# Router logits taken out of the attention's projections, and rows queued without their norm

## The reference, cut to what matters

```python
xn  = layernorm(x)                       # (x - mean) / sqrt(var + 1e-5)
h   = rmsnorm(xn, ln1_w)                 # v * rsqrt(mean(v*v) + 1e-5) * w
q, k, v = split(h @ wqkv.T); rotary on q and k; causal softmax, 16 query and 4 key heads of 16
x2  = xn + attn @ wo.T
h   = rmsnorm(x2, ln2_w)
p   = softmax(h @ gate_w.T)              # 8 experts; the two largest of a token, weights rescaled to sum 1
out = x2 + sum over the token's two experts e of  w_e * (silu(h @ w1_e.T) * (h @ w3_e.T)) @ w2_e.T
x   = x + out
```

## Time and profile before

| | |
|---|---|
| median of 3 runs | 1738.77 us (1736.22 to 1740.03) |
| the profiled execution's own time | 1730.77 us |
| its span (first to last instruction) | 1729.1 us |
| TensorE busy | 1624.7 us, 94% |
| VectorE busy | 1166.1 us, 67% |
| ScalarE busy | 931.3 us, 54% |
| GpSimd busy | 556.0 us, 32% |
| granted TensorE clock, mean | 0.968 |
| routing (stage7) up to the first expert product | 1212.6 to 1345.5 us |
| experts (stage8) | 1345.5 to 1729 us |

### The profile page before, as it was taken

The page is one execution under the profiler, slowest core; times in us unless marked ns, Lnnn a source line. Parts: engine busy times, 40 slices in busy tenths (PEclk is TensorE's granted clock), DMA queues, the critical chain, the costliest instruction groups (busy, mean ns, idle before and its releaser), DMA issues. The chain is left out here.

```text
span 1729.1 us, 29571 instructions
## 1 busy us (share of the span) xinstructions
PE 1624.7 (94%) x9040; PEld 807.7 (47%) x9040; DVE 1166.1 (67%) x3195; ACT 931.3 (54%) x2069; POOL 556.0 (32%) x842
## 2 busy tenths in 40 slices
PE   7899989899999999999999999998995899999996
PEld 3367655333333333334333343332884455565554
DVE  6722788899888888888888888870685344343342
ACT  6134544166676776676676766667573333333332
POOL 3530338163515003030030300000377344444443
PEclk9999999799999999999999999999895899999999
DMA  5000000311030300303003030000378677777774
GB/s 165 1 7 19 2 1 7 62 36 28 2 62 2 62 2 1 62 2 62 2 1 62 2 62 2 1 1 1 120 234 276 122 129 130 131 130 129 129 126 71
DMA packets 252195, 105.77 MB, mean 61 GB/s; under 512 B 208064, under 2 KB 247880, under 8 KB 252040
## 3 DMA queue, kind: packets, MB, share of 16 engines
q1 hardware_dynamic: 233296, 80.62, 22.0%
q0 software_dynamic: 13392, 18.49, 6.3%
q10 hardware_dynamic: 5352, 4.76, 0.8%
HBM read 30.88 MB, written 23.67 MB: 32 GB/s over the span
## 5 line engine op out<-in xcount | busy, mean ns | idle before, releaser
L1677 ACT ACTIVATE prob<-pS 128x512 f32<-128x512 f32 (+3 forms) x1280 | 582.3, 542 | 267.5 <-PE pS L1563 176.2
L1734 DVE TENSOR_REDUCE mx<-pM 128x1 f32<-128x512 f32 x768 | 501.6, 685 | 71.3 <-PE pM L1543 68.1
L1543 PE MATMUL pM<-KT,QT 96*128 96x512 bf16 (+3 forms) x1280 | 434.1, 356 | 16.5 <-DVE mx L1734 5.5
L1559 PE MATMUL pS<-QT,KT 99*128 99x512 bf16 (+3 forms) x1280 | 422.9, 352 | 6.8 <-ACT prob L1677 1.8
L2440 PE MATMUL bank<-w13T,QKV 128*128 x568 | 257.2, 596 | 15.4 <-ACT QKV L2467 15.4
L1730 DVE CUSTOM_DVE_ANT_0 junk<-pM,mask_row 128x128 bf16<-128x128 f32 (+3 forms) x512 | 239.9, 483 | 41.7 <-PE pM L1543 41.1
L1578 PE MATMUL pO<-prob,VV 128*32 128x512 f32 (+3 forms) x2560 | 267.8, 536 | 0.0
L1543 PEld LDWEIGHTS pM<-KT,QT 96*128 96x128 bf16 x1280 | 124.5, 98 | 208.5 <-DVE mx L1734 79.1
L1468 POOL CAST mpart<-mneg 128x16 bf16<-128x16 f32 x32 | 6.8, 213 | 653.9 <-DVE mneg L1742 653.9
L1559 PEld LDWEIGHTS pS<-QT,KT 99*128 99x128 bf16 x1280 | 123.6, 97 | 184.0 <-ACT prob L1677 140.2
L2500 DVE TENSOR_TENSOR QKV<-QKV,bank 128x512 f32<-128x512 f32 x71 | 48.8, 687 | 235.5 <-issue 200.2
(11 more groups left out here) (356 smaller groups left out, 1947.3 us busy)
## 6 DMA issues: line engine op xcount, KB each, us to landing
raw<-in_ffn_w_dram SPq DMA_DIRECT2D x48, 256.0 KB, 4.0
QKV<-queue SPq DMA_DIRECT2D x71, 136.0 KB, 2.5
out_dram<-x ACTq DMA_DIRECT2D x8, 512.0 KB, 4.7
x<-_attn_hidden_states_dram SPq DMA_DIRECT2D x14, 256.0 KB, 5.5
QKV<-QKV SPq DMA_TRANSPOSE x142, 3.2
QT<-mrow SPq DMA_DIRECT2D x128, 3.0 KB
out_dram<-QKV POOLq DMA_INDIRECT x71, 3.9
wc_s<-in_attn_Wc_dram SPq DMA_DIRECT2D x1, 1024.0 KB, 8.1
```

The source lines that it names most:

```text
L1543: last = nc.tensor.matmul(pM[:, bank, 0:w], QT[0:ROWS, par, h, qt * P:(qt + 1) * P], KT[0:ROWS, par, 512 * part:512 * part + w], start=Tru ...
L1559: last = nc.tensor.matmul(pS[:, p % NSC, lo:512], KT[0:ROWS + 3, par, kt * P:(kt + 1) * P], QT[0:ROWS + 3, par, h, 512 * c + lo:512 * c + ...
L1677: nc.scalar.activation(prob[:, n % RING, h, lo:512], pS[:, p % NSC, lo:512], ACT.Exp, scale=SCALE).then_inc(s.head_exp, 1)
L1734: nc.vector.reduce_max(mx[:, h, qt, part:part + 1], pM[:, plan.bank[item], 0:w], AX.X).then_inc(s.unit_max, 1)
```

## The change

It does these things:

1. **The router's logits become eight columns of each projection.** The logits of x2 = xn + attn @ wo.T are xn @ G + attn @ (wo.T @ G), with G the router's weights times the second norm's. G, with its mean taken away, becomes eight columns of `wqkvT` (so that stage6 projects 392 columns), and the product of `wo` with G eight columns of `woT` (so that routing projects 264). stage4 makes both: one product and one subtraction on 8 rows on VectorE, one more `turn_weight` iteration, one iteration with four small products (`output_gate`). A record of `QKV` grows to 392 words. In routing, `routed` on VectorE scales the first part into the last eight columns of `xl`, and the add of 264 columns gives rows and logits at once. `residual_norm` makes the factor for this with two more products on GpSimd.
2. `turn_h`, `h_out` and `logits` are gone, with their PSUM banks and the scaled `gws` of routing. `pX` now has three slots of a bank each, and the add waits tile by tile.
3. **The rows are queued as they are.** `records` is gone. The second norm's weights go into `w13T`: a tile of it is now copied out by two scaled activations (one per half of the channels) in place of one copy. The row's factor `rnorm` travels in the record beside the shares (`tail` is a word wider), is the scale of the silu, and is multiplied into the share.
4. **The lists are one beat shorter** (`LATE` is 10) and ordered anew. The squares of a beat are taken in the same beat, behind its add; the choice is made one beat later instead of two; the weights start one beat earlier. On ScalarE the normalised rows of the next beat stand behind this beat's squares.
5. The broadcast of the second norm's weights at stage6's start is gone; one to eight rows stands in stage4. `xl` lies in the room of `w2T`, so the first tile of `w2T` waits for the last add.

The diff's core (lines that only carry names, sizes or semaphores along are left out):

```diff
@@ stage4
+                nc.vector.tensor_tensor_reduce(scaled[0:E, 3, :], raw[0:E, 5, :], ln2_e[:, :], 1.0, 0.0, ALU.mult, ALU.add,
+                                               wsum[0:E, 0, 3:4]).then_inc(s.w_times, 1)
...
+                nc.vector.tensor_scalar(scaled[0:E, 4, :], scaled[0:E, 3, :], wsum[0:E, 1, 3:4], None,
+                                        ALU.subtract).then_inc(s.w_ready, 1)
...
+                def output_gate():
+                    pe.wait_ge(s.wT_out, 6)
+                    for m in range(C):
+                        for c in range(C):
+                            last = nc.tensor.matmul(pQK[:, 1, m * E:(m + 1) * E], raw[:, 3 + c, m * P:(m + 1) * P],
+                                                    v.gws[:, c, :], start=(c == 0), stop=(c == C - 1))
@@ stage6
-                            last = nc.tensor.matmul(pS[:, t % NSC, 0:QKVW], xT[:, i % 2, j, c, :], wqkvT[:, c, :],
+                            last = nc.tensor.matmul(pS[:, t % NSC, 0:QKVW + E], xT[:, i % 2, j, c, :], wqkvT[:, c, :],
@@ stage7
-    LATE = NQ + 3
+    LATE = NQ + 2
-            per = [0, 0, 4, 4, 4, 4, 4, 4, 8, 8, 8]
+            per = [0, 4, 4, 4, 4, 4, 4, 8, 8, 8]
@@ route_pool
             def scatter(q, first, count):
                 if first == 0:
-                    pool.wait_ge(s.h, G * q + G)
                     pool.wait_ge(s.share, q + 1)
                     pool.wait_ge(s.slots, q + 1)
...
+            for beat in range(LATE):
+                if beat >= 2:
+                    scatter(beat - 2, 0, 4)
+                if beat < NQ:
+                    root2(beat)
+                if beat >= 2:
+                    scatter(beat - 2, 4, 4)
@@ route_pe
             def project(i):
                 pe.wait_ge(s.aT_out, i + 1)
-                if i >= 2:
-                    pe.wait_ge(s.x2, 2 * i - 2)
                 for j in range(2):
+                    t = 2 * i + j
+                    if t >= SX:
+                        pe.wait_ge(s.x2, t - SX + 1)
                     for c in range(C):
-                        last = nc.tensor.matmul(pX[:, 2 * (i % 2) + j, :], aT[:, i % 2, j, c, :], v.woT[:, c, :],
+                        last = nc.tensor.matmul(pX[:, t % SX, :], aT[:, i % 2, j, c, :], v.woT[:, c, :],
...
-                    if 1 <= beat <= NQ:
-                        turn_h(2 * (beat - 1) + j)
...
-                    if 1 <= beat <= NQ:
-                        logits(2 * (beat - 1) + j)
...
-                if 2 <= beat <= NQ + 1:
+                if beat >= 2:
                     ranks(beat - 2)
                 turn_weights(ws[3 * quarter:])
-                if beat == 3:
+                if beat == 2:
                     spare_tokens()
@@ route_act
+                        for c in range(C):
+                            last = nc.scalar.activation(
+                                w13T[:, c, 2 * P * n:2 * P * (n + 1)].rearrange("p (a n) -> p a n", a=2), src[:, c],
+                                ACT.Copy, scale=v.ln2c[:, c:c + 1])
...
-                for j in range(2):
-                    if beat < NQ:
-                        attended_out(2 * beat + j)
-                    if 1 <= beat <= NQ:
-                        h_out(2 * (beat - 1) + j)
-                    weights_out(ws[j * quarter:(j + 1) * quarter])
-                    if j == 0 and 2 <= beat <= NQ + 1:
-                        exponential(beat - 2)
-                    if j == 0 and beat < NQ:
-                        normal(beat)
+                if beat < NQ:
+                    attended_out(2 * beat)
+                if beat == 0:
+                    normal(0)
+                weights_out(ws[0:quarter])
+                if beat < NQ:
+                    attended_out(2 * beat + 1)
+                weights_out(ws[quarter:2 * quarter])
+                if beat < NQ:
+                    squares(beat)
                 if 1 <= beat <= NQ:
-                    squares(beat - 1)
+                    exponential(beat - 1)
                 weights_out(ws[2 * quarter:3 * quarter])
+                if beat + 1 < NQ:
+                    normal(beat + 1)
...
                 weights_out(ws[3 * quarter:])
@@ route_dve
+                nc.vector.tensor_tensor(QKV[:, t, 0:H + E], xl[:, t % G, :], pX[:, t % SX, :], ALU.add).then_inc(s.x2, 1)
+
+            def routed(q):
+                four = slice(G * q, G * q + G)
+                if q >= 1:
+                    dve.wait_ge(s.x2, G * q)
+                nc.vector.tensor_tensor(xl[:, :, H:H + E], QKV[:, four, ROUTED:ROUTED + E], bc(v.norm1[:, 0, four]),
+                                        ALU.mult).then_inc(s.routed, 1)
...
-                if 2 <= beat <= NQ + 1:
-                    soften(beat - 2)
-                    records(beat - 2)
-                    choose(beat - 2)
-                if beat == 4:
+                if beat == 3:
                     spare_out()
                 if beat < NQ:
                     attended(beat)
-                if 2 <= beat <= NQ + 1:
+                if beat + 1 < NQ:
+                    routed(beat + 1)
+                if 1 <= beat <= NQ:
+                    soften(beat - 1)
+                if beat >= 2:
                     settle(beat - 2)
                 if beat == 2:
                     spare_hot()
+                if 1 <= beat <= NQ:
+                    choose(beat - 1)
                 if beat < NQ:
                     residual(beat)
@@ stage8
         def silu(j):
             act.wait_ge(s.half, j + 1)
+            act.wait_ge(s.tail_in, j + 1)
             if j >= 2:
                 act.wait_ge(s.gated, j - 1)
-            nc.scalar.activation(sil[:, j % 2, :], pH[:, j % 2, 0, :], ACT.Silu).then_inc(s.sil, 1)
+            nc.scalar.activation(sil[:, j % 2, :], pH[:, j % 2, 0, :], ACT.Silu,
+                                 scale=share[:, j % RT, E + 1:E + 2]).then_inc(s.sil, 1)
```

More of the change, by code:

```diff
@@ L44 @@
 QKVW = (NH + 2 * NKV) * HD
+ROUTED = QKVW
 E = 8
@@ L852, in weight_rows @@
         def weight_rows(n):
-            return E if n == 5 else P
+            return E if n >= 5 else P
         with nc.Block() as block:
@@ L932, in turn_weight @@
                         pe.wait_ge(s.wT_out, n - 1)
-                    src = scaled[:, n, :] if n < 3 else raw[0:rows, n, :]
+                    src = scaled[:, n, :] if n < 3 else raw[:, n, :] if n < 5 else scaled[0:rows, n - 2, :]
                     for c in range(C):
@@ L1795, in stage7 @@
     NQ = T // G
-    LATE = NQ + 3
+    LATE = NQ + 2
     R = 4
+    SX = 3
     RP = 3
@@ L1933, in route_pool @@
             pool.wait_ge(s.ids_in, 2)
-            for beat in range(1, LATE):
-                if beat >= 3:
-                    scatter(beat - 3, 0, 4)
-                if beat <= NQ:
-                    root2(beat - 1)
-                if beat >= 3:
-                    scatter(beat - 3, 4, 4)
+            for beat in range(LATE):
[5 more added lines that the diff above has]
+                    scatter(beat - 2, 4, 4)
             pool.wait_ge(s.acc_in, 16 * NQ)
@@ L2157, in soften @@
                 nc.vector.tensor_tensor(pr[:, :, :], lg[:, :, :], bc(red[:, 0, :]), ALU.subtract).then_inc(s.soft, 1)
-            def records(q):
-                dve.wait_ge(s.square, G * q + G)
-                dve.wait_ge(s.rstd2, q + 1)
-                dve.wait_ge(s.hT_mm, 2 * q + 2)
-                dve.wait_ge(s.resid, q + 1)
-                for t in range(G * q, G * q + G):
-                    nc.vector.scalar_tensor_tensor(out=QKV[:, t, 0:H], in0=QKV[:, t, 0:H],
-                                                   scalar=rstd[:, 4, t:t + 1], in1=v.ln2_b[:, :], op0=ALU.mult,
-                                                   op1=ALU.mult).then_inc(s.h, 1)
             def choose(q):
@@ L2235, in route_dve @@
             nc.vector.memset(prior[:, 0, :], 0.0).then_inc(s.prior0, 1)
[L2236 to L2239 removed]
+            routed(0)
             for beat in range(LATE):
[L2241 to L2245 removed]
+                if beat == 3:
                     spare_out()
@@ L2355, in stage8 @@
     xq, xqT = carve(R, REC), carve(2, C * P)
-    tail = carve(RT, E + 1).bitcast(I32)
+    tail = carve(RT, E + 2).bitcast(I32)
     share = tail.bitcast(F32)
```

149 lines of the change are left out of this document (65 added, 84 removed).

## The result

The changed kernel takes 1752.46 us (median of five, 1750.69 to 1758.83); the kernel before, beside it, 1736.97 us. The ratio is 1.0090, with a 95% interval of 1.0069 to 1.0111: 12 to 19 us slower. The forecast was 1750.2 us (1739 to 1760), slower with 0.78. The profiled execution is the first of the five (1752.84 us, span 1751.1).

A forecast was written before the change was run, and what follows sets the result against it. POOL's scatter queue was taken as the bound, overtaken by a new ScalarE-TensorE loop of 13.25 us a beat. The last scatter came 10.9 us later, plus 0.5 in attention: 1738.77 + 11.4 = 1750.2 us, range 1739 to 1760.

The forecast's parts named there:

- What bounds: Routing: POOL's queue of 64 scatters ends last, 11.7 us a beat; the experts' stage only moves as a whole.
- Rival 4: Routing: the squares' wait is in truth covered and the change moves nothing, 1738.8 us; chance 0.03.
- rival 1: Routing: POOL stays the bound because the clock holds and the loop is 11.5 us; 1738.9 to 1742 us; chance 0.20.
- The loop: Routing: ScalarE and TensorE take turns instead of overlapping, 11.5 us a beat, 13.25 with the lowered clock.
- only then the copy: ScalarE's queue: next attended tiles are copied only behind squares, exponential, rows and two weight tiles; TensorE waits, idling nearly 5 us.
- Its size: Loop per beat: ScalarE's part 6.05 us, TensorE's 5.45, lowered clock 1.75; together 13.25 us.
- Rival 2: Routing: TensorE stays at half clock through its whole part, a beat of 15.6 us, 1764 us; chance 0.10.
- Rival 1's rule: Routing: removed records, with two SBUF inputs, no longer contend with POOL's reads, giving the lower end, 1738.9 us.
- Beat 3: Routing: spare-token products ahead of this beat's transposes add 1.3 us, last add at 1258.8 us.
- The tail: Routing's end: from beat 5's scatters POOL bounds, 11.7, 10.2 and 8.9 us, last scatter starting at 1345.7 us.
- rival 3: Routing's end: tables end last, their ranks standing behind 46 weight tiles; 2 to 6 us more, 1752 to 1756; chance 0.05.
- What was costed at nothing: Silu's scale and wait, router's product and small transposes, and work removed from TensorE, ScalarE and VectorE: 0 us directly.

The follow-up runs named there:

- e4: Kernel before with only ScalarE's order taken from the change (squares of the same beat, next beat's normalised rows behind them): 1758.45 us, ratio 1.0119.
- e10: Changed kernel with only ScalarE's list reordered: weight tiles and next attended copy ahead of the squares; spare-token products left in place: 1744.17 us, ratio 1.0059.
- e9: Changed kernel, ScalarE's weight tiles and next attended copy ahead of the squares, spare-token products behind the fifth beat's first transposes: 1738.65 us, ratio 1.0015.
- e1: Changed kernel with ScalarE's copy of the next beat's first two attended tiles ahead of this beat's squares: 1757.20 us, ratio 1.0120.
- e7: Changed kernel with both lists regrouped: ScalarE copies, squares, rows, then weight tiles; TensorE projections, transposes, then weight tiles: 1765.71 us, ratio 1.0167.
- e5: Changed kernel with nine unused products a beat on TensorE, ahead of the weight tile in its pause: 1745.78 us, ratio 1.0052.
- e6: Changed kernel with the spare-token products and what follows from them one beat later: 1751.47 us, ratio 1.0086.
- e12: Changed kernel, ScalarE reordered, spare tokens later, ranks between projections, slots ahead of adds, first-layer weight tiles spread evenly: 1735.44 us, ratio 1.0005.
- e2: Changed kernel with nine unused products a beat on TensorE, behind the weight tile: 1757.77 us, ratio 1.0125.
- e3: Changed kernel with one unscaled 512-wide copy per first-layer weight tile in place of two scaled halves: 1753.70 us, ratio 1.0099.

## Why the prediction was right, step by step

**What bounds.** Right: POOL's chain sets the start of the experts, and the experts' stage moved as a whole. Rival 4, a covered wait, is out; so is rival 1 as the changed kernel stands, since POOL waited ahead of every beat and the clock did not hold.

**The loop.** Right in kind. That squares of the same beat and rows behind them make two engines take turns is shown from both sides: e4 closes the loop with nothing but the order; e10 opens it with nothing but the order (12.3 us a beat from the second scatter beat to the fifth, for 13.6), and e9, with the spare tokens moved too, brings routing back to 134.0 us. The step "only then the copy" was too narrow: the weight tiles' waits for evictions are a second string (e1, e7).

**Its size.** ScalarE's part 6.05, measured 5.7; TensorE's 5.45, measured 5.7 at full clock (e5); the clock 1.75, measured 2.1. Together 13.25, measured 13.6 in the beats without other work. Rival 2, half clock throughout, is out in these beats, as the second projection ran at 1.00; but beat 3, behind the spare tokens, ran at 0.50 from 1252 to 1262 us, through its transposes and its first projection. That one row of a pause priced the clock so well is partly luck: in e9, a pause of 2.09 us left the next weight tile at half clock, and one of 2.10 us a beat later left it at full clock.

```profile
1274.36 1.06 PE L2014 MATMUL bank<-ident,raw 128*128 128x128 f32 x4 [2.09 <-ACT w13T L2086]
...
1285.88 0.63 PE L2014 MATMUL bank<-ident,raw 128*128 128x128 f32 x4 [2.10 <-ACT w13T L2086]
```

**Rival 1's rule.** The records went, and with the loop open POOL did reach 11.8 and 11.5 us a beat in e9 (scatter beats 3 to 5, 1270.10 to 1293.43). By the Trainium skill, SBUF — State Buffer (Who interferes with whom), a VectorE instruction with two SBUF inputs contends with GpSimd's reads, so that is what one would expect without the records. No run took them alone out of the kernel before, so their share is open. It bought no time.

**The sum.** Relative to the first transposes, the forecast had the last scatter start at 133.1 us; it was 141.1, 8.0 more. Three terms were too small:
- Beat 3: 1.3 us were charged for the spare tokens, as an addition. They cost 3.5 (17.1 for 13.6), since TensorE waits for VectorE's columns and then works at half clock (e6). But moving them away gained only 1.7 us of routing (e6), so this term and the next do not simply add.
- The tail: "from there POOL bounds", 30.8 us from the sixth scatter beat to the last scatter. It was 34.2: POOL waited 0.93 and 2.33 us for slots, as the ranks of the last beats stand behind weight tiles, and these wait for their transfers (TensorE's and VectorE's rows below). That is rival 3's mechanism with another end: the slots were late, not the tables.
- Beats 1 and 4 to 7: 0.3 to 0.7 us each, together 1.9.

```profile
1343.82 1.12 PE L2014 MATMUL bank<-ident,raw 128*128 128x128 f32 x4 [0.42 <-DMA raw<-in_ffn_w_dram]
...
1345.44 0.61 PE L1997 MATMUL bank<-QKV,ones 128*128 128x32 f32 x2
```

```profile
1346.09 0.19 DVE L2207 SCALAR_TENSOR_TENSOR place<-iota,bank 128x32 f32<-128x32 f32 x1 [6.38 <-PE bank L1997]
```

So routing grew by 18.8 us between the two profiles where 10.9 were forecast. That the median came within 2.3 us of the forecast is partly chance: the medians differ by 15.5, less than the profiles (22.1), as the profiled execution of before was itself below its median, and one profile of each does not tell what routing took in the other executions. The 0.5 us charged to the stages ahead cannot be checked: they vary by 7 us. The 1.2 us of the wider projections, from which it comes, holds: from the first to the last of them it is 56.9 us, for 55.6. In rival 1, four beats of 11.7 us from 1256.25 end at 1303.05, not 1303.4; nothing hangs on it.

**What was costed at nothing** held, as a sum: the silu's scale, wider adds and projections, logits as columns, unscaled records. e9 and e12 carry them all, at 1.0015 and 1.0005 of the kernel before. Equally, the transposes, copies and records that went bought nothing that e12 shows; that this is because they were beside POOL's queue fits its rows before, where from the second beat on it waits 0.30 us ahead of a beat's first scatter, and was not tested by itself.

## What to carry to other kernels

Read an in-order engine's list for loops: when an instruction that waits for another engine's last result stands ahead of what that engine needs next, the two take turns, however much work was removed; look for every such string, and a pool of banks that the waiting engine frees is one. Check too that a wait on such a pool asks for no more than the pool needs. Price the pause in the waiting engine's clock too, not in its idle time alone. Before removing work, ask which queue sets the end; here sixteen products, eight transposes and four records a beat bought nothing that could be measured.

## What the runs showed of the hardware that was not expected

Work that nothing uses made the kernel faster: nine products a beat kept the granted clock at 1.00, for 0.50, and took routing from 151.8 to 144.6 us (e5); the same products one weight tile later took it to 153.7 (e2). The clock was at 0.50 after two pauses of 2.02 and 2.44 us with 0.63 us of transposes between them. A pause made shorter by 0.5 us on ScalarE gave nothing, as the next projection ran slower by 0.4 (e3). And pauses of one length did not have one price: of two of 2.1 us in e9, the clock was at 0.50 behind one and at 1.00 behind the other.
